# A Perceiver-style two-layer block on one core: cross-attentions that begin with V and K of two batches

## The reference

```python
x = x + xattn0(layernorm(x), ctx, ctx, Wq, bq, Wk, bk, Wv, bv, Wo, bo)   # 16 heads of 16
x = x + attn0(layernorm(x), w_Q, w_K, w_V)
x = x + experts(layernorm(x), router_w, w_gate, w_up, w_down)            # 8 experts, top 2
x = x + xattn1(layernorm(x), ctx, ctx, Wq, Wo)       # K = ctx @ Wq.T and V = ctx @ Wq.T
x = x + attn1(layernorm(x), W_qkv, W_out)            # rotary, causal
x = x + ternary_linear(layernorm(x), weight)

def xattn(q, k, v, ...):
    q, k, v = (split_heads(t @ W.T + b) for t, W, b in ...)
    attn = softmax(q @ k.T * 16 ** -0.5)
    return merge_heads(attn @ v) @ Wo.T + bo
```

## Time and profile before

| | before |
|---|---|
| median of three runs | 2792.21 us |
| profiled execution | 2789.23 us |
| its span | 2787.4 us |
| TensorE busy | 2515.0 us, 90% |
| VectorE | 1788.0 us, 64% |
| ScalarE | 1231.2 us, 44% |
| GpSimd | 796.2 us, 29% |
| mean granted clock of TensorE | 0.958 |

### The profile page before, as it was taken

How to read it: one execution, slowest core, us unless ns; L and a number is a source line. 1 busy time by engine, 2 the same in 40 slices (tenths; PEclk the granted TensorE clock), 3 DMA queues, 4 the chain that set the end, 5 groups by cost and what they waited for, 6 DMA issues and landing times. The chain is left out here.

```text
span 2787.4 us, 101550 instructions
## 1 busy us (share of the span) xinstructions
PE 2515.0 (90%) x44320; PEld 1970.7 (71%) x44320; DVE 1788.0 (64%) x3820; ACT 1231.2 (44%) x2700; POOL 796.2 (29%) x696
## 2 busy tenths in 40 slices
PE   7999999999979866999996788889898799999997
PEld 6878788887845544666664677767776688888885
DVE  5666666666647754111112688888877778888886
ACT  5555555555534523222222566666664323333332
POOL 3222222222221211333333433333321232333321
PEclk9999999999989967999998899999999899999998
DMA  5333333333313113111112577676665100000000
GB/s 189 102 95 100 101 84 98 101 102 95 90 39 109 45 43 129 45 44 42 44 44 79 174 213 210 193 209 194 198 192 137 66 3 3 10 10 10 10 10 25
DMA packets 154328, 256.90 MB, mean 92 GB/s; under 512 B 24344, under 2 KB 102300, under 8 KB 144672
## 3 DMA queue, kind: packets, MB, share of 16 engines
q1 hardware_dynamic: 147072, 233.62, 28.6%
q0 software_dynamic: 6816, 16.79, 1.9%
HBM read 149.78 MB, written 57.80 MB: 74 GB/s over the span
## 5 line engine op out<-in xcount | busy, mean ns | idle before, releaser
L795 POOL TENSOR_TENSOR ctxT_x_lo<-ctx_in_x,ctxT_x_hi 128x514 fp32r<-128x514 f32 x256 | 306.4, 1198 | 890.6 <-ACT ctxT_x_hi L613 890.5
L671 DVE TENSOR_REDUCE neg_max_x<-ps_score_x 128x2 f32<-128x514 f32 x512 | 330.2, 686 | 303.3 <-PE ps_score_x L527 302.4
L635 ACT ACTIVATE prob_x<-ps_score_x,neg_max_x 128x257 f32<-128x257 f32 x1024 | 403.6, 480 | 227.5 <-DVE neg_max_x L671 227.5
L538 PE MATMUL ps_v_x<-v_wide_x,probT_x 128*32 128x68 f32 x18432 | 334.4, 225 | 71.8 <-DMA v_wide_x<-v_out_x 33.0
L538 PEld LDWEIGHTS ps_v_x<-v_wide_x,probT_x 128*32 128x32 f32 x18432 | 290.2, 109 | 147.1 <-issue 92.5
L695 DVE STREAM_TRANSPOSE probT_x<-prob_x 128x1152 f32<-128x1152 f32 x256 | 342.2, 1337 | 0.0
L2067 POOL TENSOR_TENSOR rot_s<-turned_s,swapped_s 128x512 f32<-128x512 f32 x128 | 163.5, 1291 | 300.1 <-DVE swapped_s L1996 255.1
L626 ACT ACTIVATE kT_x<-ps_x,bias_k 128x257 f32<-128x257 f32 x256 | 122.1, 477 | 234.8 <-PE ps_x L223 234.7
L1617 DVE TENSOR_TENSOR hid_moe<-ps_up_moe,silu_moe 128x512 f32<-128x512 f32 x71 | 49.1, 692 | 253.1 <-PE ps_up_moe L1429 253.1
L223 PE MATMUL ps_x<-ctxT_x_hi,w_v_x_hi 128*128 128x288 f32 x512 | 167.7, 328 | 25.5 <-DVE attn_x L715 13.7
L527 PE MATMUL ps_score_x<-kT_x,q_x 32*64 32x257 f32 x4096 | 178.0, 402 | 4.8 <-ACT prob_x L635 4.1
(11 more groups left out here) (241 smaller groups left out, 5697.3 us busy)
## 6 DMA issues: line engine op xcount, KB each, us to landing
ctx_in_x<-ctx SPq DMA_DIRECT2D x64, 1028.0 KB, 5.8
v_wide_x<-v_x SPq DMA_DIRECT2D x512, 76.5 KB, 2.1
v_out_x<-v_x SPq DMA_DIRECT2D x128, 306.0 KB, 3.7
v_wide_x<-v_out_x SPq DMA_DIRECT2D x512, 76.5 KB, 2.7
w_moe<-moe_experts SPq DMA_DIRECT2D x8, 1536.0 KB, 9.7
y_in_x<-y_out SPq DMA_DIRECT2D x16, 512.0 KB, 5.1
v_wide_s<-v_s SPq DMA_DIRECT2D x32, 136.0 KB, 2.5
X<-x SPq DMA_DIRECT2D x8, 512.0 KB, 12.5
```

Source lines behind the costliest of these rows:

```text
L538: ins = pe.do.matmul(self.ps_v[r * T:(r + 1) * T, b % 2, :, :], self.probT[b % 3][:, r, n * T:(n + 1) * T], self.v_wide[b % 4][:, :, r, n, ...
L635: act.do.activation(self.prob[b % 3][:, r, 0:S], self.ps[:, r, 0:S], ACT.Exp, bias=self.neg_max[b % 2][:, r:r + 1]).then_inc(*s.exp.at(tag ...
L671: dve.do.tensor_reduce(self.neg_max[b % 2][:, r], self.ps[:, r, 0:S], AX_X, ALU.max, negate=True).then_inc(*s.neg_max.at(tag, b, half))
L795: pool.do.tensor_tensor(self.ctxT[b % 3].lo[:, :, 0:S], self.ctx_in[g % 2][:, :, j, :], self.ctxT[b % 3].hi[:, :, 0:S].bitcast(F32), ALU.s ...
```

## The change

Nothing is computed otherwise; instructions change places. All of it is in the two cross-attentions.

1. The start: V and K of batches 0 and 1 now come before the turns and queries of group 0, on all engines. What only V and K need (weights, context 0, the first two splits) no longer waits for the tables and biases.
2. SP's loads in the start: first the weights of K and V and context 0; then x, tables, biases and the weights of Q in `x0`, or the experts' quarter 0 in `x1`; then the output weights and context 1. `load_y(1)` now stands right behind context 1, ahead of every `leave_v`.
3. `add_y` takes a step: one of its four instructions per iteration, in `j` 0 to 3 for quarter 1 and `j` 8 to 11 for the later ones.
4. LayerNorm of the next group moves four iterations later: statistics in `j` 5 and 6, root in 6, scaling in 7, turns in 8 and 9, queries in 12 and 13.

The diff, with one line around each edit:

```diff
@@ -126,7 +126,7 @@
         self.w_in = {}
-        for tag, names in (("x0", "qkvo"), ("s0", "qkv"), ("moe", ("router",)), ("x1", "qo"),
+        for tag, names in (("x0", "kvqo"), ("s0", "qkv"), ("moe", ("router",)), ("x1", "qo"),
                            ("s1", ("qkv0", "qkv1", "qkv2", "out"))):
@@ -178,7 +178,7 @@
                 "x_turned", "x_inT", "gate_ps", "up_ps", "silu", "hid", "hid_turned", "hidT", "y_ps", "y"))
-        self.y_in, self.y_scaled, self.y_added, self.y_first = count("y_in", grid(s, range(2)), 16), count("y_scaled", grid(s[1:], range(2))), count("y_added", grid(s[1:])), count("y_first", grid(range(2)))
+        self.y_in, self.y_scaled, self.y_half, self.y_added, self.y_first = count("y_in", grid(s, range(2)), 16), count("y_scaled", grid(s[1:], range(2))), count("y_half", grid(s[1:])), count("y_added", grid(s[1:])), count("y_first", grid(range(2)))
 
@@ -398,7 +399,8 @@
         self.v_is_k = "v" not in mats
-        self.matrices = [n for n in "qkv" if n in mats]
+        self.matrices = [n for n in "kvq" if n in mats]
+        self.of_ctx, self.of_x = (["q"], []) if self.v_is_k else (["k", "v"], ["q"])
         self.w = {n: Weight(nc, stack, s, tag, n, mats[n], [sb(f"w_in_{n}", [P, KD * D])]) for n in self.matrices}
@@ -412,9 +414,6 @@
         s, tag = self.s, self.tag
-        for n in self.matrices:
-            self.w[n].load(sp)
-        sp.do.dma_start(self.w_out[:, :, :], self.w_out_dram).then_inc(*s.w_in[tag, "o"].at(0))
 
@@ -458,13 +457,22 @@
 
+        for n in self.of_ctx:
+            self.w[n].load(sp)
+        load_ctx(0)
+        if self.first:
+            load_constants, load_x = self.first
+            load_constants(sp)
+            self.w["q"].load(sp)
         if self.y_in:
             load_y(0)
-        load_ctx(0)
+        sp.do.dma_start(self.w_out[:, :, :], self.w_out_dram).then_inc(*s.w_in[tag, "o"].at(0))
         load_ctx(1)
+        if self.y_in:
+            load_y(1)
         if self.first:
             for i in range(1, SG):
-                self.first(sp, i)
+                load_x(sp, i)
         for i in range(B + 1):
@@ -473,8 +481,6 @@
                 place_v(i)
-            if self.y_in and i == 0:
-                load_y(1)
             if self.y_in and i % BPS == 4 and i // BPS + 2 < SG:
@@ -560,16 +566,17 @@
 
-        for k in range(KD):
-            self.ln.turn(pe, 0, k, banks)
-        for m in range(KD):
-            project_q(0, m)
         for b in range(2):
...
                 project_k(b, m)
+        pe.wait_ge(s.const_in, "o")
+        for k in range(KD):
+            self.ln.turn(pe, 0, k, banks)
+        for m in range(KD):
+            project_q(0, m)
         for i in range(B + 6):
@@ -586,10 +593,10 @@
                 project_out((i - 11) // 8)
-            if n < SG and j in (4, 5):
-                self.ln.turn(pe, n, j - 4, banks)
             if n < SG and j in (8, 9):
-                project_q(n, j - 8)
+                self.ln.turn(pe, n, j - 8, banks)
+            if n < SG and j in (12, 13):
+                project_q(n, j - 12)
 
@@ -635,17 +642,20 @@
 
+        for n in self.of_ctx:
+            self.w[n].split_hi(act)
+        for b in range(2):
+            ctx_hi(b)
+        for n in self.of_x:
+            self.w[n].split_hi(act)
         act.wait_ge(s.const_in, "o")
-        for n in self.matrices:
-            self.w[n].split_hi(act)
+        k(0)
+        k(1)
         for piece in range(KD):
             self.ln.keep_hi(act, 0, piece, banks)
-        for b in range(3):
-            ctx_hi(b)
+        ctx_hi(2)
         for m in range(KD):
             q(0, m)
-        k(0)
-        k(1)
         for i in range(B + 6):
@@ -654,11 +664,11 @@
                 k(i + 2)
-            if n < SG and j in (4, 5):
+            if n < SG and j in (8, 9):
                 act.wait_ge(s.q_ps, tag, n - 1, KD - 1)
-                self.ln.keep_hi(act, n, j - 4, banks)
-            if n < SG and j in (8, 9):
-                q(n, j - 8)
+                self.ln.keep_hi(act, n, j - 8, banks)
+            if n < SG and j in (12, 13):
+                q(n, j - 12)
 
@@ -721,7 +731,6 @@
 
-        dve.wait_ge(s.const_in, "o")
         for t in self.ctxT:
@@ -730,6 +739,9 @@
         ins.then_inc(*s.pad.at(tag))
+        for n in self.of_ctx:
+            self.w[n].split_lo(dve)
+        dve.wait_ge(s.const_in, "o")
         if self.biases:
@@ -746,15 +758,16 @@
             self.ln.take_stats(dve, 0, j)
+        for n in self.of_x:
+            self.w[n].split_lo(dve)
+        dve.wait_ge(s.pad, tag)
+        turn_v(0)
         self.ln.scale(dve, 0)
-        for n in self.matrices:
-            self.w[n].split_lo(dve)
+        lead = 1 if self.v_is_k else 2
+        for b in range(1, lead):
+            turn_v(b)
         for piece in range(KD):
             self.ln.keep_lo(dve, 0, piece, banks)
-        dve.wait_ge(s.pad, tag)
-        lead = 1 if self.v_is_k else 2
-        for b in range(lead):
-            turn_v(b)
         for i in range(B + 6):
@@ -771,16 +784,16 @@
                 turn_prob(i - 1)
-            if n < SG and j in (4, 5):
+            if n < SG and j in (8, 9):
                 dve.wait_ge(s.q_ps, tag, n - 1, KD - 1)
-                self.ln.keep_lo(dve, n, j - 4, banks)
-            if n < SG and j in (1, 2):
+                self.ln.keep_lo(dve, n, j - 8, banks)
+            if n < SG and j in (5, 6):
                 dve.wait_ge(s.x_in[1], SG - 1)
...
                 for half in range(GPS // 2):
-                    self.ln.take_stats(dve, n, (j - 1) * (GPS // 2) + half)
-            if n < SG and j == 3:
+                    self.ln.take_stats(dve, n, (j - 5) * (GPS // 2) + half)
+            if n < SG and j == 7:
                 self.ln.scale(dve, n)
@@ -795,35 +808,38 @@
 
-        def add_y(i):
-            g = slice(i * GPS, (i + 1) * GPS)
-            pool.wait_ge(s.y_in, i, 1)
-            for n in range(2):
-                y = self.y_in[:, n, :, :]
-                ins = pool.do.tensor_tensor(y, y, self.share[:, n, g].unsqueeze(2).to_broadcast([P, GPS, D]), ALU.mult)
-            ins.then_inc(*s.y_scaled.at(i, 0))
-            pool.wait_ge(s.y_scaled, i, 0)
-            pool.do.tensor_tensor(self.X[:, g, :], self.X[:, g, :], self.y_in[:, 0, :, :], ALU.add).then_inc(*s.y_scaled.at(i, 1))
-            pool.wait_ge(s.y_scaled, i, 1)
-            pool.do.tensor_tensor(self.X[:, g, :], self.X[:, g, :], self.y_in[:, 1, :, :], ALU.add).then_inc(*s.y_added.at(i))
+        def add_y(i, step):
...
+            g, n = slice(i * GPS, (i + 1) * GPS), step % 2
+            y = self.y_in[:, n, :, :]
+            if step < 2:
+                pool.wait_ge(s.y_in, i, 1)
+                pool.do.tensor_tensor(y, y, self.share[:, n, g].unsqueeze(2).to_broadcast([P, GPS, D]), ALU.mult).then_inc(
+                    *s.y_scaled.at(i, n))
+            else:
+                pool.wait_ge(s.y_scaled, i, 1)
+                if n:
+                    pool.wait_ge(s.y_half, i)
+                pool.do.tensor_tensor(self.X[:, g, :], self.X[:, g, :], y, ALU.add).then_inc(*(s.y_added if n else s.y_half).at(i))
 
...
         ins.then_inc(*s.v_zero.at(tag))
+        for b in range(2):
+            ctx_lo(b)
         pool.wait_ge(s.const_in, "o")
         self.ln.root(pool, 0)
-        for b in range(3):
-            ctx_lo(b)
-        if self.y_in:
-            add_y(1)
+        ctx_lo(2)
         for i in range(B + 6):
...
                 ctx_lo(i + 3)
-            if n < SG and j == 2:
+            if n < SG and j == 6:
                 self.ln.root(pool, n)
-            if n + 1 < SG and j == 8 and self.y_in:
-                add_y(n + 1)
+            if n == 1 and j < 4 and self.y_in:
+                add_y(1, j)
+            if n + 1 < SG and 8 <= j < 12 and self.y_in:
+                add_y(n + 1, j - 8)
             if self.biases and i % 8 == 4 and i >= 12:
@@ -2104,21 +2120,17 @@
 
-        def run(stage, first=None):
+        def run(stage):
 
...
                     pe.do = eng
-                    if first:
-                        pe.wait_ge(s.const_in, "o")
                     stage.tensor(pe)
...
                     sp.do = eng
-                    if first:
-                        first(sp)
                     stage.sync(sp)
@@ -2137,8 +2149,8 @@
         with ExitStack() as own:
-            run(CrossAttention(nc, own, s, "x0", X, a["ctx"], consts, {n: a["x0_" + n] for n in "qkvo"}, biases, load_x),
-                load_constants)
+            run(CrossAttention(nc, own, s, "x0", X, a["ctx"], consts, {n: a["x0_" + n] for n in "qkvo"}, biases,
+                               (load_constants, load_x)))
         with ExitStack() as both:
...
             with ExitStack() as own:
```

## The result

The changed kernel takes 2773.03 us (median of 4 runs, 2770.93 to 2775.51), the kernel before, measured beside it, 2790.15 (4 runs, 2787.71 to 2792.39): a ratio of 0.9934, 95% interval 0.9914 to 0.9953. Measured twice more, it gave 0.9951 (0.9932 to 0.9971; 2781.69 against 2790.62) and 0.9958 (0.9936 to 0.9979; 2780.16 against 2791.46). By these ratios it is faster by 0.4 to 0.7%, 12 to 18 us, where 2777 us and 13.2 us less were forecast. The kernel before was run again beside every group of experiments, each group on another chip, so ratios are compared and not times of different groups. The profiled execution took 2775.51 us, its span 2773.7, 13.7 less than before.

The account below looks back on a forecast made before the run. It took TensorE, busy 90% of the span, to bound the kernel. Its terms, 2.7 + 2.0 + 11.5 - 3 = 13.2 us off 2789.2, gave 2776.0, forecast as 2777, with the range 2766 to 2787.

Parts of the forecast that it names:

- The hole: Cross-attention 1, batch 3's context split: TensorE's 11.31 us wait for GpSimd goes, 11.5 us off, bounds 10.5 and 13.
- The first start: Start of cross-attention 0: V and K first bring batch 0's scores to 26.6 from 29.3, 2.7 us off.
- the landings: Start of cross-attention 0: K and V weights and first context land by about 7, x by 8.5, biases by 11.
- K's second half waits about 0.3: Start of cross-attention 0: K waits about 0.3 us for VectorE, in its statistics, to hand on banks; included.
- the clock: Start of cross-attention 0: TensorE at 1.2 GHz for batch 0's V and K, to 15.9, then at 2.4 GHz.
- The 1.5 us of ScalarE's last copy: Start of cross-attention 0: ScalarE's last piece after the queries, 1.45 us, counted ahead of the scores.
- The second start: Start of cross-attention 1: K of two batches ahead of the turns, scores earlier, 2.0 us off.
- the low end: Start of cross-attention 1: 0.7 us off, scores at 1527.8, if K's work has not raised TensorE's clock.
- the lock: Start of cross-attention 1: VectorE's eight adds beside GpSimd's two context splits would lose about 1.5 us; outside the sum.
- The delay of LayerNorm: Loops of both cross-attentions: LayerNorm and queries four iterations later cost 0 in 0, 0.4 per group in 1, 3 us.

Follow-up runs that it names:

- The controls: The changed kernel itself, unaltered, measured again in two later groups against the kernel before: 0.9951 (2781.69 us) and 0.9958 (2780.16 us).

## Why the prediction came out

**The hole (11.5 us off forecast) was right, in place, size and cause.** First group 87.5 to 76.2 us, forecast 75 to 76; no wait of TensorE for GpSimd is left. The controls' profiles gave 79.7, with the late scalings shown above, and 76.1. The experiments add what the forecast hadn't seen: the change fills the hole three times over.

**The first start (2.7 off forecast) was wrong in sign.** Over the profiles taken with each, the old start gives 29.0 us (29.3, 29.3, 29.1, 28.0, 29.2) and the new one 30.4 (28.5, 30.4, 30.9, 31.1, 31.1): 1.4 us later, by five profiles each. The steps that failed are the landings and the term "K's second half waits about 0.3" for VectorE. The biases were there at 13.6 and not 11, so LayerNorm was ready at 19.1 and not at 16.8, and the statistics, which stand behind them, let V's transposition begin only at 16.8: TensorE waited 1.21 us for the bank in the first profile and 2.05 to 2.60 in the four others. Of the biases' 2.6 us some 1.4 can be SP's issues (1.78 and 0.52 us for the last two instead of 0.43 each); the rest is in the transfer itself, behind 1.5 MB of loads, and no run divides it further.

V began 1.2 us later than forecast: its context was split from 9.4 on, where the forecast had it landed by 7, a figure of which 1.5 MB at 430 GB/s and the first issue give only 4.3. V's 1.2 us and the bank's 0.9 are about what the first profile missed 26.6 by, 1.9 us. In four of five profiles the clock, taken to be high from 15.9 on, added to it. The 1.5 us of ScalarE's last copy were in the forecast and came.

**The second start (2.0 off forecast) gave nothing.** Scores at 28.6, 28.8, 28.8 and 28.4 us with the old order, at 29.2, 28.1, 29.2, 28.1, 29.2 and 29.2 with the new: 28.6 and 28.8 on the mean. The results landed 1.2 later (9.2 against 8.0), as forecast, which put the turns at 17.7 us after the start; they came at 18.9, since the adds lost 1.24 us to the splits, which the forecast had left outside its sum. The rule that it weighed there, the Trainium skill's ("SBUF — State Buffer", section "SBUF: two separate sides"), says that VectorE's instructions with two SBUF inputs and GpSimd's that read SBUF exclude each other for a whole instruction; by it the forecast had estimated about 1.5. The trace agrees with 1.24: the first two of the eight adds end just behind the two splits (0.68 and 1.51 us), the other six take 0.47 or 0.48, and the memsets, which read nothing, cost the adds nothing. The level did rise behind K, at 14.9, but fell at 18.3, in TensorE's idle 3.43 us. It came back at 25.3 in the two profiles with 28.1, and at 28.1 to 28.6 in the four with 29.2. Chosen for the sum was 2.0, "nearer to the low end" of 0.7 to 4.3; the low end less the lock, -0.5, is what came.

**The delay of LayerNorm (3 us on forecast) is open in size, and its mechanism was another.** In the first profile six groups cost 0.5 us in all. The waits for `weighed` moved as said, from iterations 2 and 6 (10.2 and 9.6 us over all groups) to 6 and 10 (8.8 and 10.3), and their sum stayed, 27.0 after 26.7; in the two controls it was 31.3 and 31.6, with the one long wait in iteration 8 shown above. The forecast had read that lock from the same rows (2.12 us of scalings beside a split) and used it for the adds alone, not for the scalings beside the weighting. Loop 1 is 611.0 us on the mean in the five profiles with that meeting, 604.9 in the five with LayerNorm late and without it, 603.2 in the three with it early: too few to tell the last two apart.

**The sum came out since the wrong terms cancel.** Forecast 2.7 + 2.0 + 11.5 - 3 = 13.2; in the profiles 0.9 - 0.6 + 11.3 - 0.5, another 3.8 off in the last group, which varies by 5 us between profiles (63.5 to 68.7) for a reason that no run shows, and 1.1 lost in what lies between: 13.7 in span. The first start's 0.9 was luck. Loop 1 is the largest of what differs between profiles: 598.5 to 612.7 us in thirteen profiles without the hole, mean 606.8, where the loop of cross-attention 0 stays within 761.0 and 761.8 in all but one (763.5). Some 6 us of this spread go with the late scalings, by the means above; the rest is open. So of before's 616.9, also one draw, some 10 us are the hole. The 12 to 18 us of the ratios hold no more than this and a rest that no run here separates.

## What to carry to other kernels

A hole with one owner is worth more than a start rebuilt: look first for the load that stands behind a store for no reason, since one moved load (0.9966) took by its median half to four fifths of the gain of the whole change (0.9934 to 0.9958). When work is moved forward, ask for each engine what the moved instruction now stands behind in its queue: a load order helps no one who stands behind another's transposition or split. Ask too which instructions of VectorE and GpSimd will now run side by side: here the scalings moved next to the weighting, and a group with such a meeting took some 5 us more. And a term that rests on one profile of a stretch whose length varies by 3 us from run to run has to carry that in its bounds.

## What the runs showed of the hardware

- Eight `scalar_tensor_tensor` of 128x256 with two SBUF inputs: 3.38 us beside a memset of GpSimd, 4.62 beside the last 1.84 us of two of its `tensor_tensor` of 128x514, 5.35 beside nearly all of both. The splits took 2.71 and 2.69 us, and 2.52 with VectorE idle.
- Four `tensor_scalar` of 128x256 with one SBUF input: 1.34 us alone, 2.12 to 2.21 beside one split of 128x514, 3.69 to 3.76 beside a split and a `tensor_tensor` of 128x1024 behind it.
- `tensor_scalar` of 128x2 beside a memset of 128x2448: 2.62 us for two, ending 0.03 us behind the memset; 0.36 with GpSimd idle.
- SP's issue of a bias's transfer took up to 1.78 us with 1.5 MB of loads issued ahead of it, and 0.43 in the kernel before.
- TensorE's granted clock fell from 2.4 to 1.2 GHz for 3.40 us at 18.40, behind a wait of 2.19 us for a bank and 0.70 us of work; behind a wait of 1.21 us at the same place, in another run of the same kernel, it stayed at 2.4.
